# One ternary matrix from VectorE instead of two sign matrices summed by TensorE

## The reference

```
scale = mean(|W|) + EPS
q = clip(round(W/scale), -1, 1) * scale          # W_up, W_gate, W_down
hidden = silu(x @ q(W_up).T) * (x @ q(W_gate).T) ; out = hidden @ q(W_down).T
```

## Time and profile before

| | us |
|---|---|
| median of 3 runs | 766.53 |
| runs | 764.83, 766.53, 767.41 |
| span of the profiled execution | 762.1 |
| TensorE matmuls busy | 718.1 (94%) |
| VectorE busy | 388.6 (51%) |
| ScalarE busy | 276.1 (36%) |
| GpSimd busy | 108.5 (14%) |

### The profile page before, as it was taken

How to read it: one execution, slowest core, us unless ns; L and a number is a source line. 1 busy time by engine, 2 the same in 40 slices (tenths; PEclk the granted TensorE clock), 3 DMA queues, 4 the chain that set the end, 5 groups by cost and what they waited for, 6 DMA issues and landing times.

```text
span 762.1 us, 11832 instructions
## 1 busy us (share of the span) xinstructions
PE 718.1 (94%) x3882; PEld 380.7 (50%) x3883; DVE 388.6 (51%) x672; ACT 276.1 (36%) x430; POOL 108.5 (14%) x154
## 2 busy tenths in 40 slices
PE   4999999999996789999994999999999999999997
PEld 2465556566464556555553444444444444444443
DVE  5568666676537855444457343453434434343223
ACT  3465554555454355222224222222222222222221
POOL 4203034033021400000005000000000000000000
PEclk9999999999998999999997999999999999999999
DMA  7983034033044396222212000020000100010001
GB/s 223 391 320 143 1 127 151 0 129 147 1 173 159 130 342 232 78 91 83 83 42 70 27 15 14 14 71 14 15 0 14 69 14 14 0 55 1 0 0 55
DMA packets 32493, 66.73 MB, mean 88 GB/s; under 512 B 6352, under 2 KB 6352, under 8 KB 31440
## 3 DMA queue, kind: packets, MB, share of 16 engines
q1 hardware_dynamic: 28464, 53.24, 20.1%
q0 software_dynamic: 4000, 13.11, 5.0%
HBM read 47.73 MB, written 18.61 MB: 87 GB/s over the span
## 4 chain that ended last, share of the span: by engine, by line
PE 85%; DVE 5%; DMA 3%; issue 2%; ACT 2%; POOL 2%; SPq 1%; DVEq 0%; POOLq 0%; ACTq 0%
PE bank L1056 31%; PE bank L1314 29%; PE bank L1324 14%; PE bank L1049 6%; PE bank L1199 2%; PE bank L1213 1%; DMA nrm<-in_L_ffn_W_down_dram 1%; PE bank L1234 1%; DMA stage<-in_L_attn_Wv_dram 1%; DVE w_att L843 1%; DVE w_att L842 1%; SPq L183 1%; POOL rs L305 1%; DVE st L568 1%; DMA n<-sorted_outputs,pos_now 0%
## 5 line engine op out<-in xcount | busy, mean ns | idle before, releaser
L1314 PE MATMUL bank<-w_att,region 128*128 128x512 f16 (+1 forms) x1024 | 233.1, 381 | 0.8 <-ACT w_att L535 0.8
L1314 PEld LDWEIGHTS bank<-w_att,region 128*128 (+1 forms) x1024 | 100.5, 98 | 120.5 <-issue 3.6
L1022 DVE SCALAR_TENSOR_TENSOR tmp<-tmp,hk,bank 128x512 f32<-128x512 f32 x64 | 47.8, 747 | 153.7 <-PE bank L1314 153.3
L1324 PE MATMUL bank<-region,tmpA 128*128 (+1 forms) x504 | 119.1, 379 | 0.0
L1056 PE MATMUL bank<-w_moe,tmpA 128*128 x456 | 104.6, 379 | 1.5 <-DVE tmpA L913 1.5
L1056 PE MATMUL bank<-xT,w_att 128*128 128x512 f16 x384 | 88.6, 387 | 4.3 <-DVE region L753 2.3
L543 ACT ACTIVATE tmp<-bank,qs 128x512 f32<-128x512 f32 x64 | 44.0, 688 | 125.1 <-PE bank L1314 125.1
L547 ACT ACTIVATE tmpA<-tmp 128x512 f16<-128x512 f32 x64 | 40.4, 631 | 121.7 <-DVE tmp L1022 121.7
L1324 PEld LDWEIGHTS bank<-region,tmpA 128*128 128x128 f16 x504 | 49.2, 98 | 59.6 <-DVE stage L1005 0.9
L1056 PEld LDWEIGHTS bank<-w_moe,tmpA 128*128 128x128 f16 x456 | 44.4, 98 | 47.1 <-issue 1.7
L1025 DVE TENSOR_TENSOR tmpA<-tmp,tmpA 128x512 f16<-128x512 f32 x64 | 44.3, 692 | 45.7 <-ACT tmpA L547 45.7
(11 more groups left out here) (134 smaller groups left out, 752.4 us busy)
## 6 DMA issues: line engine op xcount, KB each, us to landing
stage<-in_L_ffn_W_up_dram SPq DMA_DIRECT2D x8, 1024.0 KB
stage<-in_L_ffn_W_gate_dram SPq DMA_DIRECT2D x8, 1024.0 KB, 7.0
sorted_tokens<-a SPq DMA_DIRECT2D x10, 512.0 KB, 10.3
n<-sorted_tokens SPq DMA_DIRECT2D x20, 256.0 KB, 2.6
stage<-in_ctx_dram SPq DMA_DIRECT2D x4, 1024.0 KB
stage<-in_L_ffn_W_down_dram SPq DMA_DIRECT2D x4, 1024.0 KB
nrm<-in_L_ffn_W_down_dram SPq DMA_DIRECT2D x4, 1024.0 KB, 7.4
out_dram<-stage SPq DMA_DIRECT2D x16, 256.0 KB, 2.1
```

The lines of the kernel that those rows point to most:

```text
L1022: dve.scalar_tensor_tensor(out=h32, in0=sil, scalar=hk[:, 0:1], in1=gate_ps[:, :], op0=ALU.mult, op1=ALU.mult).then_inc(s["hid_mul"], 1)
L1314: mm = pe.matmul(dst, w[:, bass.ds(cf_c, 1), k * P:(k + 1) * P].rearrange("p a n -> p (a n)"), x3T[:, bass.ds(b, 1), i, k].rearrange("p a ...
L1324: mm = pe.matmul(ffy_ps[t][:, :], hid[:, parity, i, t * P:(t + 1) * P], tern[2][:, bass.ds(c, 1)].rearrange("p a n -> p (a n)"), start=(st ...
```

## The change

VectorE's second comparison goes first and writes 1 where the weight is below the lower threshold (it no longer multiplies by -1). Then VectorE waits for that result, compares with the upper threshold and subtracts the first result in the same instruction, which writes +1, 0 or -1. TensorE turns this one matrix, with one matmul to a block. Nothing else differs: the number of VectorE instructions, the buffers, the semaphores and their counts stay.

```diff
@@ signs_of (VectorE)
-            dve.tensor_scalar(signs[:, j, 0], unit_slot[j], thr[:, 0, j:j + 1], None, ALU.is_gt).then_inc(s["sign_a"], 1)
-            dve.tensor_scalar(signs[:, j, 1], unit_slot[j], thr[:, 1, j:j + 1], -1.0, ALU.is_lt,
-                              ALU.mult).then_inc(s["sign_b"], 1)
+            dve.tensor_scalar(signs[:, j, 1], unit_slot[j], thr[:, 1, j:j + 1], None, ALU.is_lt).then_inc(s["sign_a"], 1)
+            wait_apart(dve, "sign_a", 3 * g + j + 1)
+            dve.scalar_tensor_tensor(out=signs[:, j, 0], in0=unit_slot[j], scalar=thr[:, 0, j:j + 1],
+                                     in1=signs[:, j, 1], op0=ALU.is_gt, op1=ALU.subtract).then_inc(s["sign_b"], 1)
@@ unit_transposes (TensorE)
-                    for h in range(2):
-
-                        mm = pe.matmul(q_ps[r][:, cut], signs[:, j, h, r, cut], ident_b[:, :],
-                                         start=(h == 0), stop=(h == 1))
+                    mm = pe.matmul(q_ps[r][:, cut], signs[:, j, 0, r, cut], ident_b[:, :], start=True, stop=True)
```

## The result

The changed kernel takes 768.51 us (median of 20 runs, 765.89 to 771.55) against 765.93 for the kernel before (20 runs, 763.25 to 768.24). The ratio is 1.0034, 95% interval 1.0021 to 1.0048: slower by 2.6 us, with an interval of 1.6 to 3.7. The forecast was +1.55 us, inside the 0.3%; the measured change is just over that bound. In a second group of 12 runs the ratio was 1.0020 (1.0008 to 1.0032). A ratio is not the quotient of the two medians, and the two can differ by some 0.1%.

The account below looks back on a forecast made before the run. The prediction took a chain of waits through VectorE's comparisons and the units' matmuls on TensorE as the bound. Its terms, 2.14 - 1.29 + 0.70 = +1.55 us on 766.53, gave 768.1 us, range 764.8 to 770.6.

Parts of the forecast that it names:

- A unit's price on VectorE: Each unit's comparisons: two-source instruction 2.35 us, wait 0.11, next operation 3.65 us after the start (+1.26).
- TensorE's 0.90: Each unit's matmuls on TensorE: sixteen hold it for 0.90 us, where 32 held it for 1.79.
- the loop of place 2: Three tile steps with a unit: loop through three engines takes 7.42 us a step, above TensorE's 6.95; -1.29 us.
- the open loop: Rival: in the tile steps the loop doesn't close, TensorE keeps its 0.90 a step; +0.1 us, 766.7 us, chance 0.07.
- the fast two-source form: Rival: VectorE's two-source comparison is as fast as the one-source one; -3.2 us, 763.3 us, chance 0.05.
- the weight loads as TensorE's pace: Rival: loading weights sets TensorE's pace, 1.63 us a unit; +3.1 us, 769.6 us, chance 0.06.
- Place 1: Last projection to first tile step: later scatters, unit loads and longer comparisons delay the th transposes; +2.14 us.
- Place 3: End of expert stage: output copy, store, gather and sum come later, units (3,1) and (3,2) hidden; +0.70 us.
- The clock rival: Rival: TensorE's low clock (1.2 GHz) lasts until the tile steps begin; +3.2 us, 769.8 us, chance 0.17.
- The base: Starting time 766.53 us, 4.4 us above the 762.1 us span; nothing of the change touches what lies outside.

Follow-up runs that it names:

- e3: Kernel before with TensorE turning only the first of the two matrices (-1 entries left out), VectorE as before: 760.68 us, ratio 0.9916.
- e2: Changed kernel with TensorE still doing two matmuls to each block, the second overwriting the first: 772.05 us, ratio 1.0056 against the kernel before.
- e4: Changed kernel with the last three units (3,0), (3,1), (3,2) done the old way on both engines: 765.95 us, ratio 0.9980 against the kernel before.
- h1: Changed kernel with four one-source bn_stats replacing the two-source comparison in four units, their weights left out: 765.29 us, ratio 0.9985 against the kernel before.
- e1: The changed kernel run again without any edit: 768.8 us, ratio 1.0020 against the kernel before.
- f1: Changed kernel with unread products filling TensorE's waits behind units (0,0), (0,1), (0,2) and (1,1): 766.62 us, ratio 1.0010 against the kernel before.
- f2: Changed kernel with unread products filling TensorE's waits behind the last three units: 768.8 us, ratio 1.0033 against the kernel before.
- f5: Changed kernel with unread products at the first place, behind the last units and between the last stage's transposes: 765.65 us, ratio 0.9994 against the kernel before.
- f3: Kernel before with unread products filling TensorE's waits behind the last three units: 765.57 us, ratio 0.9990.
- g1: Changed kernel with one VectorE instruction a unit (bf16 rounding, sign in ScalarE's copy): 759.12 us, ratio 0.9913 against the kernel before; again 760.38 us, 0.9901.
- g2: g1 with unread products in TensorE's waits at the first place and up to and between the last stage's transposes: 756.97 us, ratio 0.9859 against the kernel before.

## Why the prediction was right, and where it was short

**A unit's price on VectorE: right.** 2.35 us for the two-source instruction (2.352 measured), a wait of 0.11, 3.65 in all (3.66). The nearest rows, L602 for the length and the column scalar's 0.06, were enough.

**TensorE's 0.90 and the loop of place 2: right.** 7.42 was summed and 7.42 measured, three times, -1.28 against -1.29. The 0.5 us of waiting forecast ahead of each unit does not show as such: the profile has one wait for the comparisons there, of 0.17, and the rest lies behind the th transposes, where the next product starts 0.55 to 0.93 after them instead of 0.44 to 0.46. e3 shows that with the short pair the loop isn't the limit (6.95), e2 that with 32 matmuls TensorE is (7.85). That rival, the open loop, is out, and so are the fast two-source form (2.35 us) and the weight loads as TensorE's pace (6.95 in e3).

**Place 1: the sum near, its make-up wrong.** +1.73 against +2.14. The queue on SyncE went on 2.28 later and not 1.26, since the last scatter was shut out; unit (1,1) then landed 5.8 us after its issue (266.39 to 272.16) where I had taken the old 7.2. One error hid the other, which is luck. That the landing could be up to 1.2 less stood in the prediction; that the scatter's issue could grow did not.

**Place 3: mis-sized, the step that failed.** I had +0.70, from the late output copy, and that part is there (2.95 to 3.66). What I called hidden, "the units (3,1) and (3,2) then hold VectorE", was priced as VectorE's own time only. GpSimd issues the gathers in that very stretch, and the two-source comparison under which the second one begins shuts it out until it has ended: 2.88 us for 0.97, so the stretch is 2.33 longer and not 0.70. e4 takes it away with the old pair, h1 with one-source work of the same length, which leaves the store late and VectorE busy. The trace of before had the sign of it: the gather of 1.47 us beside L843, the next two at 0.97 and 0.95, and a scatter of 2.09. The Trainium skill has a rule for this ("SBUF — State Buffer", section "SBUF: two separate sides"): VectorE and GpSimd share one pair of ports as an exclusive lock, which whichever starts first holds for its whole instruction. On VectorE's side that goes for an operation in a mode that uses both ports, which also locks out the writing of descriptors for a DMA issued by GpSimd, and for one with two SBUF inputs, there only against a GpSimd operation that reads SBUF. By that rule an issue that is held waits for the whole instruction, and the trace agrees: it ended 0.85 after L844. Whether an indirect DMA's issue is such a read the section does not say, and which port or which mode it is no run here shows; h1 shows that it hangs on the kind of VectorE work and not on its length.

**Not foreseen: +0.46** between th of tile 3 and the comparison of (3,0). It is there in the kernels whose steps wait for VectorE (93.20 to 93.25 in the changed kernel, e1, e4, f1, f2, f5 and h1) and absent where TensorE sets the pace (92.74 to 92.78 in before, e2, e3, f3, g1 and g2). All of it lies between th of tile 3 and the product behind it, 0.93 us instead of 0.46 (302.82 to 303.28 in the kernel before). The rows after the change:

```profile
302.78 0.61 PE L1050 MATMUL bank<-ident,tmp 128*128 128x128 f32 x4
...
303.71 2.76 PE L1057 MATMUL bank<-w_moe,tmpA 128*128 x12 [0.33 <-issue]
```

The profile shows nothing that TensorE waited for there ("issue"). That the engine's own preparation of the next product is laid bare when it has just been waiting is argued, not shown.

**The clock rival: half right.** I gave it 0.17 as the whole outcome. It is a matter of the single execution, with 0.9 us in e1's profile (8.30 instead of 7.42), and it also strikes with the old units (8.63 in f3). The 20 runs of the changed kernel show the same: the seven with a mean granted clock of 0.972 took 765.9 to 767.5 us, the four at 0.966 took 770.1 to 771.5. f1 suggests that it adds 1 to 2 us to the changed kernel's median.

**The account of the 2.6 us.** The table's 3.24 is the forecast 1.55, less 0.41 at place 1, plus 0.01 at place 2, 1.63 at place 3 (the gathers) and 0.46 for the bare issue. That is the difference of two profiles, each of an execution faster than its kernel's median; the medians differ by 2.6. How much of the 2.6 is the clock's is open.

**The base.** I took the 4.4 us between the span and the median as lying outside the span. Every run has only 1.6 to 1.8 us between its time and its core's span; the rest was that the profiled execution was a fast one. That the forecast of 768.1 came within 0.4 of the measured 768.51 is partly luck as well: the base of three runs was 766.53 and the median of 20 is 765.93.

## What to carry to other kernels

Price a longer VectorE instruction by its neighbours too: a DMA that GpSimd began to issue while VectorE read two SBUF tensors was issued only after that instruction's end in every case here (2.88 us for 0.97). Taking work from the busiest engine is worth only what the loop through the other engines leaves: sum that loop, edge by edge, before counting the saving. And when two instructions have to become one, look for arithmetic that does it with one source (rounding by the output type, the clip in a copy that runs anyway): it was worth 6 us here where the two-source form cost 2.6.

## What the runs showed that I had not expected

GpSimd's indirect DMA took 0.94 to 1.08 us to issue when left alone, and up to 3.35 us when it met a two-source VectorE instruction and a one-source comparison behind it. Four bn_stats of the same length left it at 0.98. One-source comparisons of 128x2048 f32 delay it as well, to 1.47 and 2.09 in the kernel before.

What counts is which kind of instruction stands where. An instruction with two SBUF sources that is running when the issue begins puts the issue's end 0.82 to 0.85 behind its own, or later where a one-source comparison follows. The short ones of 128 x 512 do it too (the fourth gather of the kernel before, 1.16 us, under L944 at 406.62). With one of the two sources in PSUM it does not: L1023 was running when an issue began at 426.80 us in the changed kernel, and the issue took 1.07 like the others of its line. One that starts later in the issue does not delay it: the last gather of the changed kernel takes 0.95, though L945 starts 0.72 into it. A one-source comparison delays it in either place: started 0.06 into the issue in the kernel before (L843 at 402.74), it puts the end 0.13 behind its own. So the last scatter was held twice, at its start by L844 and at its end by L842.

Products that nobody reads held TensorE at 2.4 GHz where they also bridged the sparse stretch right ahead of the dense one, as in f5 (1.00 in every stretch read). f2 bridged the long wait alone, and the clock fell 1.4 us before it was needed (0.88 in 420 to 422 us, last stage from 422.92).
